# A fused AdaLN and quantised FFN on one core: x turned by VectorE instead of TensorE, the bias added by ScalarE, w_gate in 12 loads, int16 weight codes, own buffers for the last tiles

## The reference, cut to what matters

```python
x = x + ffn(cond(x, cats, W, b), w_gate, w_up, w_down)     # x: 32 x 128 x 512 f32
def cond(x, cats, W, b):                                   # W: 64 x 512 x 512, one matrix for each batch
    return einsum('bsd,bdh->bsh', x, W[cats]) + b[cats][:, None, :]
def ffn(x, w_gate, w_up, w_down):                          # w_gate, w_up: 1536 x 512, w_down: 512 x 1536
    x = act_qdq(x)                                         # scale from max |x| over the whole tensor, 16 bits
    up, gate = act_qdq(x @ lpbq_dequant(w_up).T), act_qdq(x @ lpbq_dequant(w_gate).T)
    gate = act_qdq(gate * fixed_qdq_u16(sigmoid(gate)))
    return act_qdq(gate * up) @ lpbq_dequant(w_down).T
def lpbq_dequant(w):                                       # 4 bits: a step for each block of 32 of a row
    s = max(max|block| / 7, 1e-12); return clip(round(block / s), -8, 7) * s
```

## Time and profile before

| | |
|---|---|
| median of 3 runs | 958.22 us (958.16 to 959.72) |
| the profiled execution | 959.29 us, of which its span 957.5 us |
| PE busy | 893.6 us, 93% |
| DVE busy | 658.0 us, 69% |
| ACT busy | 420.9 us, 44% |
| DMA | 254.32 MB, mean 266 GB/s |
| first stage (cond) | from the start to about 141 us |

### The profile page before, as it was taken

How to read it: one execution, slowest core, us unless ns; L and a number is a source line. 1 busy time by engine, 2 the same in 40 slices (tenths; PEclk the granted TensorE clock), 3 DMA queues, 4 the chain that set the end, 5 groups by cost and what they waited for, 6 DMA issues and landing times. The chain is left out here.

```text
span 957.5 us, 13114 instructions
## 1 busy us (share of the span) xinstructions
PE 893.6 (93%) x4736; PEld 477.3 (50%) x4736; DVE 658.0 (69%) x792; ACT 420.9 (44%) x454; POOL 3.1 (0%) x12
## 2 busy tenths in 40 slices
PE   8999999999999999999999999990079999999998
PEld 7999994444444444444444444440034444444443
DVE  2349869655667454379899889669998887755511
ACT  1112326323223223299798882229865544444000
POOL 0000000000000000000000000000000000000000
PEclk9999999999999999999999999995579999999999
DMA  8999872453574343499999735999977999987221
GB/s 320 401 397 328 321 258 100 149 165 137 163 242 131 136 142 128 172 347 421 400 398 390 262 124 208 404 421 414 418 274 293 328 342 341 337 289 281 88 88 66
DMA packets 81587, 254.32 MB, mean 266 GB/s; under 512 B 32082, under 2 KB 32082, under 8 KB 77714
## 3 DMA queue, kind: packets, MB, share of 16 engines
q1 hardware_dynamic: 46354, 198.72, 55.3%
q10 hardware_dynamic: 35200, 55.20, 16.4%
HBM read 173.94 MB, written 73.66 MB: 259 GB/s over the span
## 5 line engine op out<-in xcount | busy, mean ns | idle before, releaser
L609 ACT ACTIVATE stage<-bank 128x512 f32<-128x512 f32 x186 | 108.6, 594 | 212.8 <-PE bank L861 162.9
L1137 DVE TENSOR_REDUCE tile_max<-stage 128x1 f32<-128x1536 f32 (+1 forms) x62 | 108.4, 1749 | 34.6 <-ACT stage L609 31.7
L859 PE MATMUL bank<-xq_head,wt_gate 128*128 (+1 forms) x336 | 127.4, 379 | 0.3 <-DVE xq_head L1124 0.3
L859 PE MATMUL bank<-xq_head,wt_up 128*128 x336 | 127.4, 379 | 0.1
L860 PE MATMUL bank<-xq_head,wt_up 128*128 x336 | 127.3, 379 | 0.0
L861 PE MATMUL bank<-xq_head,wt_up 128*128 x336 | 127.3, 379 | 0.0
L861 PE MATMUL bank<-xq_head,wt_gate 128*128 (+1 forms) x336 | 127.3, 379 | 0.0
L860 PE MATMUL bank<-xq_head,wt_gate 128*128 (+1 forms) x336 | 127.3, 379 | 0.0
L773 PE MATMUL bank<-xt,w_ring 128*128 128x128 f32 x960 | 112.1, 275 | 0.0
L773 PEld LDWEIGHTS bank<-xt,w_ring 128*128 128x128 f32 x960 | 109.9, 192 | 0.0
L1017 DVE SCALAR_TENSOR_TENSOR wparts<-wf,scal,wparts 128x512 f16<-128x512 f32 (+2 forms) x36 | 27.0, 749 | 62.8 <-ACT wparts L552 62.8
(11 more groups left out here) (205 smaller groups left out, 1368.7 us busy)
## 6 DMA issues: line engine op xcount, KB each, us to landing
up_ring<-up_scratch SPq DMA_DIRECT2D x54, 768.0 KB, 7.2
w_ring<-in_L_cond_W_dram SPq DMA_DIRECT2D x30, 1024.0 KB, 7.3
gate_scratch<-stage ACTq DMA_DIRECT2D x32, 768.0 KB, 3.4
gate_ring<-gate_scratch SPq DMA_DIRECT2D x32, 768.0 KB, 8.6
up_scratch<-stage ACTq DMA_DIRECT2D x30, 768.0 KB, 7.8
product_scratch<-prod_ring SPq DMA_DIRECT2D x19, 768.0 KB, 9.7
back_ring<-product_scratch SPq DMA_DIRECT2D x19, 768.0 KB, 13.0
gate_even<-gate_scratch SPq DMA_DIRECT2D x16, 768.0 KB, 8.4
```

The costliest lines, as they stand in the source:

```text
L609: nc.scalar.activation(stage[:, q % 2, n % PIECE_TILES, :], up_bank(i, n), ACT.Copy)\
L859: nc.tensor.matmul(bank, w_hi, x_hi, start=(k == 0), stop=False)
L1137: V.tensor_reduce(tile_max[:, side, bass.ds(Q * i + q, 1)], stage[:, q % 2, :, :].rearrange("p t c -> p (t c)"), AX.X, ALU.max, apply_abso ...
```

## The change

Five things are changed.

- **x.** Each batch of x is loaded by four DMAs, one for each quarter of the 512 columns, into 32 partitions each, in runs of 512 bytes: four row groups of 32 lie side by side in a partition. VectorE turns it with one 128x512 transpose of 32x32 blocks straight from `x_ring` into `xt` (now a ring of 4, `XT`), three batches ahead of the matmuls (`turn_x`, on VectorE). TensorE's transposes and ScalarE's copies are gone.
- **Bias.** ScalarE adds it, in 4 instructions of 128x128 for each batch; the last chunk's stays on VectorE.
- **w_gate** comes in 12 loads of 256 KB, one with each of the batches 5 to 16 (`GATE_AT`), the steps are made at batch 16 (`STEPS_AT`), and slices are quantised at batches 17 to 28 (`QUANT_AT`); before, at batches 16 to 27. The chunk's maximum is taken one batch later.
- **Weight codes.** `quantise_slice` writes its first product to an int16 tile `wq`, so the write rounds, and the rounding instruction is gone.
- **The end.** The residual rows of the last two tiles are loaded together into `x_tail` in the last chunk, well ahead, and the results go to `y_tail`. The last tile is matmuls of 256 columns into two banks, and each half is finished and stored by itself. The start also has 9 and 4 spare matmuls in place of 8 and 5.

The core of the diff (the branches of `turn_w` that wait for `last_copied`, the semaphore names and the placing of tiles are left out):

```diff
             def load_x_batch(i, r, first):
...
-                sp.dma_start(x_ring[:, r, :],
-                             x_flat[bass.ds(b, 1), :, :].rearrange("a s d -> (a s) d")).then_inc(x_in[r], 16)
+                for q in range(QUADS):
+                    sp.dma_start(x_ring[32 * q:32 * q + 32, r, :, :],
+                                 x_flat[bass.ds(b, 1), :, q * P:(q + 1) * P].rearrange("a (t p) j -> p (a t) j", p=32))\
+                        .then_inc(x_in[r], 16)
...
+                    if isinstance(i, int) and 0 <= BPC * i + r - GATE_AT < WSLICES:
+                        n = BPC * i + r - GATE_AT
+                        sp.dma_start(wf[:, n, :], wg_view[:, n, :]).then_inc(wgate_in[n // SLICES], 16)
...
-            def copy_xt(i, r, first):
+            def add_bias(i, r):
                 b = BPC * i + r
-                act.wait_ge(x_turned, b + 1)
-                if not first or r >= 2:
-                    act.wait_ge(cond_done, b - 1)
-                nc.scalar.activation(xt[:, r % 2, :, :], psum[4 + r % 2][:, :].rearrange("p (k s) -> p k s", k=KH),
-                                     ACT.Copy).then_inc(x_copied, 1)
+                halved = isinstance(i, int) and b < HALVED
+                act.wait_ge(cond_done, b + 1)
+                for m in range(KH):
+                    src = (half_bank(r, m) if halved else psum[r])[:, m * S:(m + 1) * S]
+                    done = nc.scalar.activation(cond_head[:, bass.ds(i, 1), m, r * S:(r + 1) * S].rearrange("p a s -> p (a s)"),
+                                                src, ACT.Identity,
+                                                bias=bias[:, bass.ds(b, 1), m:m + 1].rearrange("p a k -> p (a k)"))
+                done.then_inc(cond_copied, 1)
...
             def cond_chunk(i, first, last):
                 for r in range(BPC):
-                    if r < BPC - 1:
-                        turn_x(i, r + 1, first)
-                    elif not last:
-                        turn_x(i + 1, 0, False)
                     cond_matmul(i, r, first, last and r == BPC - 1)
...
+            def turn_x(i, r, ahead):
+
+                j, slot = i + (r + ahead) // BPC, (r + ahead) % BPC
+                dve.wait_ge(x_in[slot], 16 * QUADS * (j + 1))
+                if not (isinstance(i, int) and BPC * i + r + ahead < XT):
+                    dve.wait_ge(cond_done, BPC * i + r + ahead - XT + 1)
+                V.transpose(xt[:, slot, :, :].rearrange("p k (t s) -> p k t s", s=32),
+                            x_ring[:, slot, :, :].rearrange("p t (j k) -> p k t j", k=KH)).then_inc(x_turned, 1)
...
-                V.tensor_tensor(by_block, by_block, blocks(wrecip, w, n), ALU.mult).then_inc(w_scaled, 1)
-                dve.wait_ge(w_scaled, count)
-                V.tensor_scalar(flat, flat, ROUND, ROUND, ALU.add, ALU.subtract).then_inc(w_rounded, 1)
+                if not isinstance(count, int) or count > 1:
+                    dve.wait_ge(w_stepped, count - 1)
+                codes = wq[:, :].rearrange("p (g e) -> p g e", e=BLOCK)
+                V.tensor_tensor(codes, by_block, blocks(wrecip, w, n), ALU.mult).then_inc(w_rounded, 1)
                 dve.wait_ge(w_rounded, count)
-                V.tensor_tensor(by_block, by_block, blocks(wstep, w, n), ALU.mult).then_inc(w_stepped, 1)
+                V.tensor_tensor(by_block, codes, blocks(wstep, w, n), ALU.mult).then_inc(w_stepped, 1)
...
+            def cond_step(i, r):
+
+                b = BPC * i + r
+                fixed = isinstance(i, int)
+                if not fixed or b + XT - 1 < B:
+                    turn_x(i, r, XT - 1)
+                if not fixed or QUANT_AT <= b < QUANT_AT + WSLICES:
+                    quantise_slice(0, b - QUANT_AT)
+                if not fixed or b >= QUANT_AT + 2:
+                    low_part(0, b - QUANT_AT - 2, b - QUANT_AT - 2)
+                if r == 1 and not (fixed and i == 0):
+                    chunk_max(i - 1)
```

More of the change, by code:

```diff
@@ L39 @@
 HALVED = 2
+QUADS = 4
+WARM_BEFORE, WARM_AFTER = 9, 4
+XT = 4
+GATE_AT = 5
+STEPS_AT = 16
+QUANT_AT = 17
 LOCAL = 4
@@ L125, in adaln_ffn @@
         y_out = place("y_out", R + 40 * K, [2, H], f32)
+        x_tail = place("x_tail", R + 30 * K, [2, H], f32)
+        y_tail = place("y_tail", R, [2, H], f32)
         C = R + 56 * K
@@ L316, in adaln_ffn @@
         y_out_done = [sem(f"y_out_done{n}") for n in range(2)]
+        xtail_in, ytail_made = sem("xtail_in"), sem("ytail_made")
+        ytail_out = [sem(f"ytail_out{n}") for n in range(3)]
+        left_done, right_done = sem("left_done"), sem("right_done")
         ky_made = sem("ky_made")
@@ L498, in finish_chunk @@
             def finish_chunk(i, pairs_left, last):
-                for r in range(BPC):
+                for r in range(BPC // 2 if last else BPC):
                     if r < pairs_left:
@@ L510, in finish_chunk @@
                                  y_out[:, r % 2, :]).then_inc(y_out_done[r % 2], 16)
-                    if not last or r < 2:
+                    if not last:
                         load_x(BPC * i + r + 2, r)
@@ L748, in _, with cond_matmul @@
             pe.wait_ge(spare_made, 1)
-            spare_matmuls(8)
-            pe.wait_ge(ident_made, 1)
-            def turn_x(i, r, first):
+            spare_matmuls(WARM_BEFORE)
+            def cond_matmul(i, r, first, last=False):
                 b = BPC * i + r
-                pe.wait_ge(x_in[r], 16 * i + 16)
-                if not first or r >= 2:
-                    pe.wait_ge(x_copied, b - 1)
-                by_part = x_ring[:, r, :].rearrange("s (p k) -> s k p", k=KH)
-                for k in range(KH):
-                    mm = nc.tensor.transpose(psum[4 + r % 2][:, k * S:(k + 1) * S], by_part[:, k, :], ident32[:, :])
-                mm.then_inc(x_turned, 1)
-            def cond_matmul(i, r, first, last=False, between=None):
-                b = BPC * i + r
-                pe.wait_ge(x_copied, b + 1)
+                pe.wait_ge(x_turned, b + 1)
                 pe.wait_ge(w_in[r], 16 * i + 16)
@@ L941, in _ @@
                         down_quarter(2 * pair + h, h, q, False)
+            for q in range(Q):
+                down_quarter(CHUNKS - 2, 0, q, False)
+            for q in range(Q):
+                last_quarter(q)
         @block.vector
@@ L1076, in _ @@
-            cond_chunk(4, 2)
-            with dve.Fori(5, CHUNKS - 1) as i:
-                cond_chunk(i, 0)
+            def cond_step(i, r):
[9 more added lines that the diff above has]
+                    chunk_max(i - 1)
+                if fixed and b < STEPS_AT + 2:
+                    for m in range(KH):
+                        if b == (GATE_AT + SLICES * m + SLICES if m < KH - 1 else STEPS_AT):
+                            gate_blocks(m)
+                    if b == STEPS_AT:
+                        dve.wait_ge(wblocks_maxed, KH)
+                        weight_steps(0, WG)
+                    if b == STEPS_AT + 1:
+                        weight_scale(0, WG)
```

240 lines of the change are left out of this document (123 added, 117 removed).

## The result

| | before | changed |
|---|---|---|
| time, median of 4 runs each, taken side by side | 958.19 us | 986.37 us |
| ratio, with its 95% interval | | 1.030 (1.025 to 1.036) |
| span of the profiled execution | 957.5 | 985.0 |
| last maximum of the first stage starts at | 141.11 | 170.23 |
| from there to the end of the span | 816.4 | 814.8 |

Forecast were 952.9 us and a range of 946.5 to 961.5. The time is 25 us above its upper end. The last two lines of the table say where to look: all 29 us are in the first stage; what follows it took 1.6 us less than before.

The account below looks back on a forecast made before the run. The prediction took TensorE to bound the first stage, with the DMA engines full as well. It summed 4.7 us from the first stage and 0.6 at the end to 5.3 less: 952.9 us beside 958.22, range 946.5 to 961.5.

Parts of the forecast that it names:

- Part 2: First-stage loads: x in 512-byte packets of 28.6 ns takes 0.92 to 0.94 us, W 2.50, a batch 3.44 us.
- rival (c): VectorE's transpose in the first stage costs two cycles an element; stage ends at 141.4, about 958.0 us; chance 0.12.
- The bound of 1.20: Upper bound in us for loading x of one batch, from 0.262 MB at the 256-byte packets' 219 GB/s.
- rival (b): First-stage quarter loads crawl: x takes 1.20 us, a batch 3.70, loads set every batch, 960.7 us; chance 0.23.
- Part 3: VectorE in the first stage: bias and rounding go, a 0.71 us transpose comes; stage ends at 136.4, 4.7 us less.
- Parts 1, 4 and 5: Transposes gone, 14.4 us off TensorE, batch 3.61; ScalarE's biases, at most 2.4 us, cost nothing; w_up and w_down rounding worth nothing.
- Part 6: Kernel's end: no wait for x_res, only a half tile after TensorE and a smaller store; 0.6 us less.

Follow-up runs that it names:

- e2: Changed kernel with x of a batch in one load into all 128 partitions, 512-byte packets, from four batches of x: 954.58 us.
- e3: Changed kernel with four x loads, each into all 128 partitions in 512-byte packets, x not laid out for the turn: 957.57 us.
- e4: Changed kernel with four x loads, each into 32 neighbouring partitions in 2 KB packets, x not laid out for the turn: 983.99 us.
- f2: Changed kernel with two x loads, each into 64 neighbouring partitions in 2 KB packets, x not laid out for the turn: 986.05 us.
- f6: e1 with W of each batch in two 512 KB loads, into partitions 0 to 63 and 64 to 127: 1022.97 us.
- e5: e1 with the VectorE transpose reading its elements contiguously in place of every fourth: 945.87 us.
- e1: Changed kernel with x of a batch in one load into 128 partitions, 2 KB packets, x not laid out for the turn: 950.79 us.
- tail_and_int16: tail_only plus weight codes rounded by writing int16, without the rounding instruction: 958.04 us.
- tail_only: Kernel before with only the new end (own tiles for the last two batches, last tile in two halves): 957.09 us.
- f5: Changed kernel with two x loads, each into every second partition in 2 KB packets, x not laid out for the turn: 952.45 us.
- f1: Changed kernel with four x loads, each into every fourth partition in 2 KB packets, x not laid out for the turn: 974.83 us.
- f3: Changed kernel with four x loads cut by rows, 32 rows and all four column quarters each, into all 128 partitions: 1030.80 us.
- f7: f3 with x loads 0 and 1 issued by SP, 2 and 3 by ScalarE: 1032.18 us.
- g2: f3 with all four x loads issued by GpSimd in place of SP: 1003.23 us.

## Why the prediction was wrong, step by step

**The step that failed is Part 2, the price of the loads with x in 32 partitions.** The prediction took 0.92 to 0.94 us for x, a batch of 3.44, from a line through packets of 256 bytes and 2 KB, and bounded it by 1.20. The line was right for what it was drawn through: 28.6 ns were forecast for 512 bytes, and 28 ns were measured where the load reaches all partitions (e2). From the landing of W of batch 2 to that of x of batch 31 the forecast had 105.1 us, and e2 took 105.3 (15.47 to 120.78); the changed kernel took 138.3.

**Where the forecast seems to fit, it is luck.** e2's stage ended at 136.5 (forecast: 136.4). But its loads came 4.1 us earlier than forecast, since SP had no extra loads to issue at the start, and it was not they that set the end: VectorE worked without a gap from 84.47 us on, and this row shows no wait for x:

```profile
124.45 1.10 DVE L989 STREAM_TRANSPOSE xt<-x_ring 128x512 f32<-128x512 f32 x1
```

Its transposes of 1.10 us took back what the loads had gained. e3 is the world of the forecast in all but the partitions: four loads, x of batch 31 landed at 125.58 (forecast: 124.9), but the stage ended at 139.84, and again no transpose after 88 us waited for x. So even with loads as forecast the change brings 1.3 us in the stage in place of 4.7, and in the whole nothing that can be told (957.57 beside 958.33). There rival (c), the slow transpose, came true: it had the stage's end at 141.4 and about 958.0.

**The bound of 1.20 failed too.** It is the price of x alone at half the pace, and it left W at 2.50. x alone came close to it (1.25 by the estimate above). But the packets of W, in flight at the same time, paid as well: 333 ns in e3, 453 in e4, 439 in the changed kernel. A batch took 4.58 us, so that x and what it does to W cost 2.08. The rival (b), quarter loads that crawl, had the right cause and the right sign, with a chance of 0.23, and only half of the mechanism: it gave 960.7 with a batch of 3.70, because in it too W paid nothing. (Its clause that it decides from x = 1.12 us on doesn't fit the forecast's own sum, in which x of batch 31 already sets the end at 0.94.) By the Trainium skill's rule in SBUF — State Buffer, section "Door 1: The DMA port swizzle", 32 neighbouring partitions, and 64 neighbouring ones no less, reach 8 of the 16 ports. The runs agree with the rule in what tells it apart: 32 neighbours 984.0, 64 neighbours 986.1, every second partition 952.5, one load of all 950.8. They go beyond it in what it costs beside other loads: 4.55 to 4.60 us a batch (f2, the changed kernel, e4), where x at half the pace gives 3.70. Why the mix costs 0.9 us more than half the pace isn't settled; f6, where W and so 80% of a batch's bytes come in such loads, was within 0.2 us of half the pace for W.

**What the prediction said of that rule.** It was left out of the sum, and kept only in rival (b), because "no row settles it", and "It would bind only while all engines are at the same quarter together". That second clause was argued, not read from a row, and e4 speaks against it: its batch of 4.60 us lost more than x at half the pace all the time would have lost.

**SP's issuing was not in the sum as a rate.** It was counted at the start (six more issues of 0.455, which are 2.7 us, where the prediction took 2.3; the first W went out at 6.05 and not at 5.5), never for the steady state. At SP's bare pace, 3.1 us from one batch to the next, it would not have changed the sum, since 3.44 is more. What the sum lacked is that SP is held at loads like these, to 0.78 us for one on average. With fast packets three more loads cost 3.0 us (e2 to e3); with slow ones taking half of them off SP brought 8 us (986.4 to 978.1).

**Part 3, the transpose.** 0.71 was forecast with an upper bound of 1.25, and 1.11 measured: rival (c), which had a chance of 0.12. It is the size of a term: worth 4.9 us where loads are fast (e5 beside e1), and hidden behind late loads in the changed kernel. The pace it was taken from, that of a contiguous f32 instruction, holds for a contiguous read (0.706); the change reads every fourth element, 16 bytes apart, which the step didn't look at. By the Trainium skill (SBUF — State Buffer, same section) the memory works in lines of 16 bytes and each access to a new line costs extra; the two transposes agree. Quantising to int16 took 0.65 and 0.69 us, 1.3 to 1.4 start to start against 1.33 forecast.

**Parts 1, 4 and 5 held.** Where nothing is late, in e5 from 29 to 60 us, TensorE has no gap, and in the whole stage it waits for ScalarE nowhere; busy time by stretch:

```profile
29.00:60.00 31.00, 31.00 (x280) 31.00 (x280) 12.46 (x12) 10.33 (x36) 0.00 (x0) 1.00 1.03 409
```

280 matmuls, 32 to a batch, make 3.54 us for each, against 3.61 forecast (the trace may lack a few records, which would make it less). ScalarE's four biases take 1.13 us, not up to 2.4. In the changed kernel TensorE did wait for them, 4.9 us in 4 times, in a stage whose loads were late; whether that cost anything I didn't test. The rounding in w_up and w_down is worth nothing (tail_and_int16).

**Part 6** forecast 0.6 us. The median of tail_only is 0.9 less, with an interval from 1.6 less to 0.1 more: it agrees, and can't be told from nothing, and tail_and_int16, with the same end, stands level with the kernel before. What the traces show of it is the 0.9 us by which the last matmul lies nearer to the end, and that from the last maximum of the first stage to the end the 17 kernels with the new end took 814.6 to 817.0 us, 815.7 in the middle, where before took 816.4.

**No version that keeps the computation clearly beats the kernel before.** tail_only is the best of them, within the uncertainty. The faster ones (945.9 to 954.6) bring x in an order in which it isn't turned rightly.

## What to carry to other kernels

Before cutting a load, ask which partitions each piece reaches, not how many: here 64 neighbours cost as much as 32, and two loads into every second one cost next to nothing (952.5 beside 950.8). Where the pieces go to neighbouring partitions, price the loads beside them too, not the pieces alone; and count what the issuing engine needs for each load as a rate against the period of the loop. When a measured time meets the forecast, see whether the wait that was forecast to end last did so. When rows neither show nor exclude a rule that speaks against the change, and its effect would be multiplied by every batch, give its case a chance to match, and look for its second victim.

## What the runs showed of the hardware

- Loads into 32 neighbouring partitions lengthened the 8 KB packets of other loads from 333 to 453 ns (e4), loads into 64 neighbours to 443 (f2); with W itself in such loads they took 580 (f6).
- A 512-byte packet took 28 ns where all partitions were reached (e2, e3), 39 in the quarter loads.
- One x load took SP, in the middle and on average from 25 to 110 us: 0.37 and 0.36 us in e1 (one load of all partitions), 0.38 and 0.45 in e3, 0.41 and 0.45 in e4, 0.49 and 0.51 in f5, 0.59 and 0.67 in f1, 0.43 and 0.78 in the changed kernel, 0.62 and 0.79 in f3. Where the average is far above the middle, SP was held at single loads.
- With f3's pattern on SP the issue of W behind it rose from 0.35 us (e3) to 1.1 in the middle; with half of the loads on ScalarE's queue (f7) it took 2.4 and more, with all of them on GpSimd's (g2) 0.33.
- A VectorE transpose of 128x512 f32 took 706 ns with a contiguous read (e5) and 1107 with a read of every fourth element (changed kernel).
